# A pipelined attention and mixture-of-experts kernel: score tiles interleaved with the output products, the causal mask moved from TensorE to GpSimd

## The chip, the cores and the metric

The kernel runs on one core of a Trainium2 chip. The metric is the device time of one execution in microseconds (us); smaller is better. Engines are called by the names of the profile: PE is TensorE (PEld its weight loads), DVE is VectorE, ACT is ScalarE, POOL is GpSimd, SP is the engine that issues the transfers.

## What is computed

Two transformer layers over 16 sequences of 512 tokens with 128 features, all in float32:

- Layer 0, attention without softmax (16 heads of 8): `q` and `k` are L2-normalized per head, `out = q (kT v) / scaling`, then the output projection and the residual.
- Layer 0, experts: 8 routed experts of which each token takes 2, and 2 shared ones, with `silu(x w1) * (x w3) w2`.
- Layer 1, attention: `softmax(q kT / sqrt(8))` with a mask, 16 heads of 8. The mask works out as causal: a query sees its own key and all earlier ones, so of the 512x512 scores of a head the part above the diagonal must count as zero.
- Layer 1, experts: RMS norm, a router, each of 16 experts takes the 512 tokens with its highest logits, `gelu`, and a gated scatter back.

## The kernel before

The 16 sequences ("batches") run as a software pipeline. In one pass through the main loop four batches are in work at once, and each engine has its own instruction stream, written out by hand; engines meet at counting semaphores only. `looped` (L262) calls two phases per pass:

- `x_phase(f, b, t, g)`: the ten experts of layer 0 for batch f (`up`, `up3`, `down`), the 40 query-major score tiles of batch b from which DVE takes row maxima (`fill`, `maxima`), the end of layer 1's attention for batch t (`t_turn`, `t_out`, then the residual, the norm and the router logits), and the first norm of batch g.
- `y_phase(b, f, r, t)`: the 40 key-major score tiles of batch b (`pair_scores`, five tiles for a pair of heads) which ACT turns into probabilities (`exps`, L981 to L989), the four products with v (`outputs(0)` to `outputs(3)`, L803, each for four heads, that is two pairs), the layer 0 attention of batch f (`f_kvq`, `f_kv`, `f_kvo`, `f_out`, `f_turn_x1`, `f_gate`), and the query, key and value projections of batch r (`r_turn`, `r_q`, `r_k`, `r_v`).

Score tiles go through three PSUM banks in turn (`ba`), so tile n waits until ACT has read tile n-3. The probabilities have three buffers of five tiles, one for each pair of heads: the exponentials of pair 3 wait for `outputs(0)`, those of pair 5 for `outputs(1)`, those of pair 7 for `outputs(2)`. `outputs(k)` writes the bank `bo`; DVE copies it to `oT` (L1352), PE transposes that back into `bo` (`turn_outputs`, L816), DVE divides by the row sums (`norm`, L1354).

The causal mask is added on PE: after each product for a diagonal block comes one more 128-column matmul of a constant (`mask_k` in L575 for the key-major tiles, `mask_q` in L580 for the query-major ones), which adds a large negative number above the diagonal, so that its exponential is zero:

```
pe.matmul(bank[:, col:col + w], lhsT=KT[0:K_ROWS, head, blk * P:(blk + 1) * P],
          rhs=QT[0:K_ROWS, head, blk * P:], start=True, stop=False)
last = pe.matmul(bank[:, col:col + P], lhsT=identb[:], rhs=mask_k[:], start=False, stop=True)
```

DVE's chain for layer 0's attention starts when ACT has squared q and k (`sq`, L998): `f_l2` sums the squares (L1153) and begins an inverse square root, `f_scale` ends it (three Newton steps of three operations on two halves each, L1160 to L1162, all with both inputs in SBUF) and scales q and k (L1169). In the order of DVE's stream `r_rest` (L1336), `outputs(0)`'s copy and the rest come behind it. POOL in this phase raises variances to the power -0.5 (`power`, L442 to L444) and splits q and k into bf16 parts (L479, L481).

Router logits of batch t: `t_stats`, `t_square` and `t_row` on DVE with two `power` calls of POOL between, then `t_turn_row` and `t_router` on PE (L713, L719) through the bank `bo`, with a copy on ACT between (L971). Before the change all of this lies in `x_phase`. At the end of `x_phase`, `turn_maxima(b, 0)` (L727) transposes the maxima of the first eight heads, ACT copies them, and SP writes them into QT (`max_dmas`, L329); the first score tile of `y_phase` waits for that transfer.

## Time and profile before

| what | value |
|---|---|
| median of 3 runs | 1927.63 us (1927.26 to 1934.12) |
| the profiled execution's own time | 1928.53 us |
| its span, first to last instruction | 1926.7 us |
| PE busy | 1563.0 us, 81% of the span, 10840 matmuls |
| DVE busy | 1219.8 us, 63% |
| ACT busy | 838.3 us, 44% |
| POOL busy | 517.3 us, 27%, 498 instructions |
| mean granted TensorE clock | 0.908 |

The profile gives busy time, but matmuls are pipelined and their ends are modelled, so the distance between two starts tells more than a duration. In the timeline a row is: start, duration, engine, line, operation, output and inputs, and in brackets how long the engine was idle before it and what released it. The main loop takes most of the span; behind it come the selection of tokens and the layer 1 experts, which the change does not touch.

### The profile page before, as it was taken

The numbers are of one execution on the slowest core, as the hardware profiler recorded it, in microseconds if no ns is written. First come the engines' busy times: TensorE is split into PE (matmuls) and PEld (weight loads), VectorE is DVE, ScalarE is ACT, GpSimd is POOL, SyncE is SP. The second block draws the span as 40 slices with busy tenths as digits, with TensorE's granted clock in tenths as the row PEclk, the third lists the DMA queues.
The fourth block names the chain that finished last, engine by engine and source line by source line (L and its number), as shares of the span: only waits on it lengthen the run. The fifth ranks groups of instructions, "written<-read, shape, count | busy, mean of one in ns | idle before, by whom it ended". The sixth has DMA issues, their size and how long they took to land.

```text
span 1926.7 us, 35198 instructions
## 1 busy us (share of the span) xinstructions
PE 1563.0 (81%) x10840; PEld 985.6 (51%) x10840; DVE 1219.8 (63%) x3591; ACT 838.3 (44%) x1755; POOL 517.3 (27%) x498
## 2 busy tenths in 40 slices
PE   3889999899999999898989898989898831257675
PEld 2455555565655555565555555555564421145554
DVE  5566859586868686867767676858583448831111
ACT  0436363635454554545454546353635323423332
POOL 1322212131303131312122222212121020028886
PEclk7879999999999999999999999999999665578978
DMA  2031121303030303030212121121203000034443
GB/s 69 2 76 49 37 64 26 80 9 83 12 77 12 77 12 82 15 74 29 61 39 50 43 46 53 36 53 36 62 22 78 13 12 0 1 66 93 88 89 60
DMA packets 83244, 90.77 MB, mean 47 GB/s; under 512 B 19520, under 2 KB 73024, under 8 KB 78528
## 3 DMA queue, kind: packets, MB, share of 16 engines
q1 hardware_dynamic: 71872, 80.76, 16.7%
q0 software_dynamic: 11264, 8.92, 3.4%
q14 instruction: 84, 0.69, 0.1%
q8 instruction: 24, 0.39, 0.1%
HBM read 58.95 MB, written 29.92 MB: 46 GB/s over the span
## 4 chain that ended last, share of the span: by engine, by line
PE 55%; DVE 18%; issue 12%; POOL 5%; ACT 5%; DMA 3%; DVEq 1%; SPq 1%; ACTq 0%; POOLq 0%
PE fa L666 7%; PE ba L573 6%; PE bo L812 6%; PE fa L660 6%; PE ba L578 5%; PE facc L676 3%; PE fa L676 3%; POOL out L545 2%; PE ba L928 2%; ACT probs L989 2%; DVE passed L1455 2%; PE ba L580 2%; PE ba L575 2%; PE bo L819 2%; DVE nm L1228 1%
## 5 line engine op out<-in xcount | busy, mean ns | idle before, releaser
L989 ACT ACTIVATE probs<-ba 128x512 f32<-128x512 f32 x640 | 330.7, 641 | 103.6 <-PE ba L575 102.8
L450 POOL TENSOR_TENSOR x<-x,gd 128x512 f32<-128x512 f32 x144 | 182.4, 1267 | 675.2 <-ACT gd L964 629.4
L573 PE MATMUL ba<-QT,KT 75*128 75x512 bf16 (+3 forms) x1024 | 253.8, 309 | 39.5 <-ACT probs L989 28.7
L578 PE MATMUL ba<-KT,QT 72*128 72x512 bf16 (+3 forms) x1024 | 248.2, 306 | 18.9 <-DVE nm L1231 12.1
L575 PE MATMUL ba<-mask_k,identb 128*128 128x128 bf16 x1024 | 194.9, 223 | 0.0
L580 PE MATMUL ba<-mask_q,identb 128*128 128x128 bf16 x1024 | 192.8, 223 | 0.0
L1228 DVE TENSOR_REDUCE nm<-ba 128x1 f32<-128x512 f32 x256 | 174.3, 681 | 27.0 <-PE ba L580 26.9
L666 PE MATMUL fa<-f_nT,w 128*128 128x512 f32 x320 | 175.3, 630 | 12.3 <-DVE hh L1220 11.9
L573 PEld LDWEIGHTS ba<-QT,KT 75*128 75x128 bf16 x1024 | 101.5, 99 | 158.5 <-ACT probs L989 107.0
L660 PE MATMUL fa<-f_nT,w 128*128 128x512 f32 x320 | 173.5, 624 | 1.2 <-ACT sc L1020 1.2
L578 PEld LDWEIGHTS ba<-KT,QT 72*128 72x128 bf16 x1024 | 101.1, 99 | 119.5 <-issue 32.3
L812 PE MATMUL bo<-probs,vp 128*32 128x512 f32 (+3 forms) x2048 | 155.2, 445 | 0.8 <-DVE ao L1361 0.8
L957 ACT ACTIVATE sil<-fa 128x512 f32<-128x512 f32 x160 | 95.6, 597 | 110.5 <-PE fa L660 110.5
L1230 DVE TENSOR_REDUCE nm<-ba 128x1 f32<-128x384 f32 x256 | 140.4, 548 | 4.7 <-PE ba L580 4.7
L964 ACT ACTIVATE gd<-facc,gates 128x128 f32<-128x128 f32 x256 | 72.9, 367 | 155.1 <-PE facc L676 155.1
L580 PEld LDWEIGHTS ba<-mask_q,identb 128*128 128x128 bf16 x1024 | 102.0, 100 | 61.2 <-issue 60.0
L1220 DVE TENSOR_TENSOR hh<-sil,fa 128x512 f32<-128x512 f32 x160 | 108.3, 677 | 16.2 <-PE fa L676 8.8
L1352 DVE COPY oT<-bo 128x512 f32<-128x512 f32 x64 | 44.1, 689 | 116.4 <-PE bo L812 115.4
L964 ACT ACTIVATE gd<-fa,gates 128x128 f32<-128x128 f32 x256 | 73.0, 368 | 92.8 <-PE fa L676 92.8
L812 PEld LDWEIGHTS bo<-probs,vp 128*32 128x32 f32 x2048 | 60.9, 111 | 97.6 <-issue 67.0
L1563 DVE TENSOR_TENSOR ysum<-ba,fb 128x512 f32<-128x512 f32 x16 | 11.1, 691 | 155.8 <-PE ba L928 155.8
L545 POOL DMA_INDIRECT out<-contrib,cur x64 | 100.7, 1573 | 30.9 <-issue 18.6
(274 smaller groups left out, 2855.3 us busy)
## 6 DMA issues: line engine op xcount, KB each, us to landing
QT<-qk_parts SPq DMA_DIRECT2D x96, 192.0 KB
KT<-qk_parts SPq DMA_DIRECT2D x96, 192.0 KB
qk_parts<-qkp SPq DMA_DIRECT2D x32, 384.0 KB, 2.5
fc<-in_L_ffn_fc_weight SPq DMA_DIRECT2D x32, 256.0 KB, 3.1
xin<-in_L_attn_x SPq DMA_DIRECT2D x16, 256.0 KB, 7.1
qk_parts<-qkp SPq DMA_DIRECT2D x16, 256.0 KB, 2.7
out<-x SPq DMA_DIRECT2D x16, 256.0 KB, 2.3
xn_rows<-row SPq DMA_DIRECT2D x16, 256.0 KB, 2.4
```

The lines of the kernel that those rows point to most:

```text
L450: pool.tensor_tensor(x1[:], x1[:], gd[:, e % 2], ALU.add).then_inc(S["s_x1g"], 1)
L573: pe.matmul(bank[:, col:col + w], lhsT=KT[0:K_ROWS, head, blk * P:(blk + 1) * P], rhs=QT[0:K_ROWS, head, blk * P:], start=True, stop=False)
L575: last = pe.matmul(bank[:, col:col + P], lhsT=identb[:], rhs=mask_k[:], start=False, stop=True)
L578: pe.matmul(bank[:, col:col + w], lhsT=QT[0:QK_ROWS, head, blk * P:(blk + 1) * P], rhs=KT[0:QK_ROWS, head, 0:w], start=True, stop=False)
L580: last = pe.matmul(bank[:, col + w - P:col + w], lhsT=identb[:], rhs=mask_q[:], start=False, stop=True)
L660: pe.matmul(fa[0][:], lhsT=w1[:, e], rhs=f_nT[:], start=True, stop=True).then_inc(S["s_h1"], 1)
L666: pe.matmul(fa[1][:], lhsT=w3[:, e], rhs=f_nT[:], start=True, stop=True).then_inc(S["s_h3"], 1)
L812: last = pe.matmul(bo[32 * j:32 * j + 32, blk * P:], lhsT=vp[:, blk, 4 * k + j], rhs=prob_block(4 * k + j, blk), start=blk == 0, stop=blk ...
L964: last = act.activation(gd[:, e % 2, q], down_bank(e - 2)[:, q * D:(q + 1) * D], ACT.Copy, scale=gates[:, q, e - 2:e - 1])
L989: act.activation(probs[:, pair % 3, f_], ba[n % 3][:], ACT.Exp, scale=SCALE).then_inc(S["s_exp"], 1)
L1228: last = dve.tensor_reduce(nm[:, 3, h:h + 1], bank[:], X, ALU.max, negate=True)
L1230: dve.tensor_reduce(nm[:, 2, h:h + 1], bank[:, 0:384], X, ALU.max, negate=True)
```

## The change

- PE no longer adds `mask_k`: each key-major block is one matmul, 64 fewer for each batch. Instead POOL zeroes the triangle in the probabilities after the exponential: `cut(b, pair)` issues one `affine_select` for each of the 40 tiles, over 128 columns for tiles 0 and 2 of a pair and over two blocks of 128 columns for the other three. `outputs(k)` waits for these cuts (`s_cut`) instead of the exponentials.
- POOL's other steps of `y_phase` are put between the cuts of its pairs.
- PE's order in `y_phase` is new: score tiles stand between the four parts of an `outputs` step and between the other steps; `turn_maxima(b, 1)` comes after five tiles instead of first.
- `t_stats`, `t_square`, `t_row`, `t_turn_row`, `t_router` and `t_logits` move from `x_phase` to `y_phase`, with buffers of their own and the bank `facc`; `turn_outputs(3)` and `norm(3)` move from the end of `y_phase` into the next `x_phase`.
- The first `up` of `x_phase` waits for the transposed input alone, not for the gate's exponential; `up3` waits for DVE's copy of the gate logits.
- ACT runs a one-column `Exp` at the start of `y_phase` and a one-column `Silu` at the start of `x_phase`.
- On SP `row_dmas` moves between the two halves of `back_dmas`.

```diff
@@ SP, main loop
                 both(max_dmas, i)
+                part_dmas(i + 1)
+                back_dmas(i + 1, 0)
                 row_dmas(i - 1)
-                part_dmas(i + 1)
-                both(back_dmas, i + 1)
+                back_dmas(i + 1, 1)
@@ POOL
+            def cut(b, pair):
+                for f_ in range(5):
+                    pool.wait_ge(S["s_exp"], FILLS * b + 5 * pair + f_ + 1)
+                    apart(pool)
+                    row_ = probs[:, pair % 3, f_]
+                    if f_ in (0, 2):
+                        block_ = row_[:, 0:P]
+                        pool.affine_select(block_, block_, [[1, P]], ALU.is_ge, 0.0, base=0, channel_multiplier=-1).then_inc(S["s_cut"], 1)
+                    else:
+                        apart_by = 384 if f_ < 4 else 256
+                        blocks = row_.rearrange("p (n k) -> p n k", k=P)[:, 0:apart_by // P + 1:apart_by // P]
+                        pool.affine_select(blocks, blocks, [[0, 2], [1, P]], ALU.is_ge, 0.0, base=0, channel_multiplier=-1).then_inc(S["s_cut"], 1)
+
             def y_phase(b, f, r, t):
                 if r is not None:
                     power(b_rs[:], b_ve[:], "s_varb", "s_rsb", r + 1)
-                if r is not None:
-                    for w in range(2):
+                for pair in range(HEADS // 2):
+                    if b is not None:
+                        cut(b, pair)
+                    if r is not None and pair in (1, 2):
+                        w = pair - 1
                         pool.wait_ge(S["s_r1"], 2 * r + w + 1)
...
-                if f is not None:
-                    power(f_rs[:, 0:Q], f_ve[:, 0:Q], "s_varf", "s_rsf", 2 * f + 2)
+                    if t is not None and pair in (3, 4):
+                        power((t_rs, t_rs2)[pair - 3][:], t_ve[:], "s_vart", "s_rst", 2 * t + pair - 2)
+                    if f is not None and pair == 5:
+                        power(f_rs[:, 0:Q], f_ve[:, 0:Q], "s_varf", "s_rsf", 2 * f + 2)
@@ PE, x_phase
                     up3(f, 0)
+                if t is not None:
+                    turn_outputs(t, 3)
                 fill(2)
@@ PE, outputs(k, *beside) and the order of y_phase
-                    pe.wait_ge(S["s_exp"], FILLS * b + 10 * k + 10)
+                    pe.wait_ge(S["s_cut"], FILLS * b + 10 * k + 10)
...
-                    last.then_inc(S["s_pv"], 1)
+                        if blk == Q - 1:
+                            last.then_inc(S["s_pv"], 1)
+                        fills(*beside[blk:blk + 1])
...
+                if_f(f_kvq, 0)
+                fills(0, 1, 2)
+                if_f(f_kvq, 1)
+                fills(3, 4)
+                if_b(turn_maxima, 1)
+                if_r(r_turn)
+                fills(5, 6, 7)
+                if_r(r_q)
+                fills(8, 9, 10, 11)
+                outputs(0, 12, 13, 14)
                 if_r(r_k)
+                fills(15, 16, 17)
+                if_b(turn_outputs, 0)
+                fills(18, 19)
                 if_f(f_kv)
+                fills(20, 21)
+                outputs(1, 22, 23, 24)
+                if_f(f_kvo)
+                if_t(t_turn_row, r)
+                fills(25, 26, 27)
+                if_b(turn_outputs, 1)
+                fills(28, 29)
+                if_f(f_out)
+                fills(30, 31)
+                outputs(2, 32, 33, 34)
+                if_t(t_router)
+                fills(35, 36)
+                if_f(f_turn_x1)
+                fills(37)
+                if_b(turn_outputs, 2)
+                fills(38, 39)
                 if_f(f_gate)
+                if r is not None:
+                    if t is not None:
+                        pe.wait_ge(S["s_l1c"], t + 1)
+                    r_v(r)
+                outputs(3)
@@ ACT, y_phase
                 if b is not None:
+                    act.activation(warm[:], m_b[:, 0:1], ACT.Exp, scale=0.0)
+                exps(0, 4)
+                if b is not None:
                     copy(nmT[:, 1], bo[:].bitcast(BF16)[0:PARTS * HEADS // 2, 0:SEQ], "s_nmt", 2 * b + 2, "s_nmT")
@@ DVE, y_phase
                 if_f(f_l2)
                 if_r(r_rest, 0)
                 if_f(f_scale)
+                if_b(outputs, 0)
                 if_r(r_rest, 1)
-                outputs(0)
-                norm(0)
+                if_t(t_stats)
+                if_b(norm, 0)
                 if_f(f_kvm)
-                outputs(1)
-                norm(1)
+                if_t(t_square)
+                if_b(outputs, 1)
+                if_t(t_row)
+                if_b(norm, 1)
                 if_f(f_x1)
-                outputs(2)
+                if_b(outputs, 2)
+                if_t(t_logits)
```

## Rows read from the trace of the kernel before

**Rows 1.** Chain that ended last, one step in two neighbouring passes: start, us, work

```profile
639.05 2.29 PE bo L812 x32
...
731.16 2.29 PE bo L812 x32
```

**Rows 2.** Busy time by stretch (boundary; y; x): length, busy by engine, clock, DMA

```profile
612.30:616.20 3.90, 3.90 (x22) 3.34 (x20) 0.65 (x4) 1.06 (x2) 1.25 (x1) 0.56 0.01 2
...
613.17:658.73 45.56, 40.85 (x351) 24.49 (x351) 25.17 (x91) 28.83 (x55) 6.83 (x7) 0.97 0.30 76
658.73:705.24 46.51, 43.44 (x266) 27.58 (x266) 42.16 (x112) 16.69 (x45) 14.35 (x12) 0.99 0.08 18
```

**Rows 3.** Timeline of PE, waits and moved steps late in the x phase

```profile
689.35 1.13 PE L666 MATMUL fa<-f_nT,w 128*128 128x512 f32 x2 [0.92 <-DVE hh L1220]
...
696.00 0.28 PE L578 MATMUL ba<-KT,QT 72*128 72x256 bf16 x1 [0.69 <-DVE nm L1231]
...
699.57 0.60 PE L716 MATMUL bo<-ident,row 128*128 128x128 f32 x4
...
702.95 1.07 PE L722 MATMUL bo<-router_w,b_nT 128*128 128x16 f32 x8 [1.21 <-ACT b_nT L971]
```

**Rows 4.** Timeline of PE, a mask matmul and the matmul behind it

```profile
618.61 0.22 PE L575 MATMUL ba<-mask_k,identb 128*128 128x128 bf16 x1
618.67 0.33 PE L573 MATMUL ba<-QT,KT 75*128 75x384 bf16 x1
```

**Rows 5.** Timeline of ACT, the table load and ten exponentials of one y phase

```profile
618.93 1.28 ACT L989 ACT_TABLE_LOAD   x1 [1.52 <-PE ba L575]
...
642.82 5.01 ACT L989 ACTIVATE probs<-ba 128x512 f32<-128x512 f32 x10 [2.70 <-PE ba L575]
```

**Rows 6.** Groups of POOL's instructions by form: busy us, mean ns | idle before

```profile
L493 POOL TENSOR_SCALAR_AFFINE_SELECT earlier_e<-earlier_e 128x128 f32<-128x128 f32 x7 | 2.0, 292 | 1.0
...
L434 POOL TENSOR_SCALAR_AFFINE_SELECT blockdiag<-blockdiag 128x128 f32<-128x128 f32 x1 | 0.4, 408 | 0.1
...
L437 POOL TENSOR_SCALAR_AFFINE_SELECT below<-below 128x64 f32<-128x64 f32 x1 | 0.3, 290 | 0.1
```

**Rows 7.** Timeline behind the main loop, DVE and POOL side by side

```profile
1568.18 0.59 POOL L491 TENSOR_SCALAR_AFFINE_SELECT same_e<-same_e 128x128 f32<-128x128 f32 x1
...
1569.85 1.30 DVE L1420 TENSOR_TENSOR gates<-logits,gmax 128x1024 f32<-128x1024 f32 x1
1570.22 1.09 POOL L491 TENSOR_SCALAR_AFFINE_SELECT same_e<-same_e 128x128 f32<-128x128 f32 x1
```

**Rows 8.** Timeline of DVE in the y phase, the chain of layer 0's attention

```profile
624.24 1.28 DVE L1153 TENSOR_REDUCE n<-sq 128x64 f32<-128x512 f32 x2 [2.26 <-ACT sq L998]
...
629.14 1.27 DVE L1162 SCALAR_TENSOR_TENSOR rn<-rt,rn 128x64 f32<-128x64 f32 x2
...
633.42 0.68 DVE L1352 COPY oT<-bo 128x512 f32<-128x512 f32 x1
```

**Rows 9.** Timeline of POOL in the same y phase

```profile
629.04 1.16 POOL L481 TENSOR_TENSOR qkp<-qkr,qkp 128x512 bf16<-128x512 f32 x1
...
646.79 1.01 POOL L444 TENSOR_TENSOR f_rs<-f_ve,mhalf 128x4 f32<-128x4 f32 x1 [11.31 <-DVE f_ve L1183]
```

**Rows 10.** Timeline of PE in the same y phase

```profile
634.15 0.66 PE L819 MATMUL bo<-ident,oT 128*128 128x128 f32 x4 [1.26 <-DVE oT L1352]
...
638.98 2.36 PE L812 MATMUL bo<-probs,vp 128*32 128x512 f32 x32
```

**Rows 11.** Timeline of DVE, the centred row of the router's input

```profile
694.17 1.11 DVE L1116 TENSOR_SCALAR row<-x,b_mv,b_sc 128x128 f32 x4 [0.19 <-DVE b_sc L1262]
```

**Rows 12.** Timeline of PE at the start of a late y phase

```profile
1449.25 0.61 PE L573 MATMUL ba<-QT,KT 75*128 75x512 bf16 x1 [3.44 <-DMA QT<-nmT]
```

**Rows 13.** Busy time by stretch behind that wait (columns as in rows 2)

```profile
1451.00:1454.00 3.00, 3.00 (x18) 2.20 (x16) 0.60 (x3) 2.66 (x6) 0.00 (x0) 0.50 0.12 36
1454.00:1457.00 3.00, 3.00 (x18) 1.72 (x16) 0.00 (x0) 1.97 (x4) 0.00 (x0) 0.75 0.00 0
```

More of the change, by code:

```diff
@@ L453, in x_phase @@
                 for e in range(U0):
-                    if t is not None and e == 5:
-                        power(b_rs[:], b_ve[:], "s_vart", "s_rst", 2 * t + 1)
                     if g is not None and e == 3:
@@ L463, in x_phase @@
                         pool.tensor_tensor(xres[:], xin[:], b_o0[:, None, :].to_broadcast([P, Q, D]), ALU.add).then_inc(S["s_xres"], 1)
-                    if t is not None and e == 7:
-                        power(b_rs2[:], b_ve[:], "s_vart", "s_rst", 2 * t + 2)
                     if f is not None and e >= 2:
@@ L721, in t_router, with turn_outputs @@
                 for q in range(Q):
-                    last = pe.matmul(bo[:, q * E1:(q + 1) * E1], lhsT=b_nT[:, q * P:(q + 1) * P], rhs=router_w[:], start=True, stop=True)
+                    last = pe.matmul(facc[:, q * E1:(q + 1) * E1], lhsT=rowT[:, q * P:(q + 1) * P], rhs=router_w[:], start=True, stop=True)
                 last.then_inc(S["s_l1"], 1)
-            T_STEPS = {1: t_turn, 2: t_out, 8: t_turn_row, 9: t_router}
+            T_STEPS = {1: t_turn, 2: t_out}
+            def turn_outputs(b, k):
+                pe.wait_ge(S["s_oT"], 4 * b + k + 1)
+                for q in range(Q):
+                    last = pe.transpose(bo[:, q * P:(q + 1) * P], oT[:, q * P:(q + 1) * P], ident[:])
+                last.then_inc(S["s_tr"], 1)
             def turn_maxima(b, half):
@@ L801, in pair_scores, with outputs @@
                         scores(pe, b, n, True)
-                def outputs(k):
-                    pe.wait_ge(S["s_exp"], FILLS * b + 10 * k + 10)
+                def outputs(k, *beside):
+                    if b is None:
+                        return
+                    pe.wait_ge(S["s_cut"], FILLS * b + 10 * k + 10)
                     if k == 0:
@@ L952, in x_phase @@
             def x_phase(f, b, t, g):
+                if f is not None:
+                    act.activation(warm[:], m_b[:, 0:1], ACT.Silu)
                 for e in range(U0):
@@ L980, in y_phase, with exps @@
             def y_phase(b, f, r, t):
-                def exps(pair):
+                def exps(first, last):
                     if b is None:
                         return
-                    for f_ in range(5):
-                        n = 5 * pair + f_
+                    for n in range(first, last + 1):
+                        pair, f_ = divmod(n, 5)
                         act.wait_ge(S["s_st"], FILLS * b + n + 1)
@@ L1294, in x_phase @@
                         maxima(b, n)
+                if t is not None:
+                    norm(t, 3)
                 for e in range(U0):
@@ L1297, in x_phase @@
                         product(f, e)
-                    if t is not None and e in T_STEPS:
-                        T_STEPS[e](t)
+                    if t is not None and e == 3:
+                        t_x3(t)
                     if g is not None and e == 2:
@@ L1370, in if_r, with if_t @@
                         step(r, *w)
+                def if_t(step):
+                    if t is not None:
+                        step(t)
                 if rest:
-                    y_rest(b, f, norm, outputs, if_f)
+                    fc.b = f
+                    if_b(norm, 2)
+                    if_f(f_logits)
+                    if_f(f_gates)
+                    if_f(f_rank)
+                    if_b(outputs, 3)
                     return
                 if_r(r_norm)
-                if_f(lambda f: f_bias(f, 0))
+                if_f(f_bias, 0)
                 if_r(r_center)
-                if_f(lambda f: f_bias(f, 1))
+                if_f(f_bias, 1)
                 if_f(f_l2)
```

186 lines of the change are left out of this document (75 added, 111 removed).

## The prediction, made before the result was known

> **What bounds the kernel now.** I read the chain of waits first, for the rhythm: the same product with v comes back after 92.1 us [rows 1], so one pass of the main loop takes 92.1 us; thirteen such passes and the halves beside them make about 14 that count. Then the busy time by stretch [rows 2]. T is the start of `turn_maxima(b, 0)`. From the first score tile of the x phase to the next T are 46.51 us, in which PE is busy 43.44 and DVE 42.16: PE bounds it, DVE nearly does. From T to the next x phase, 45.56 us, PE is busy 40.85 by a generous measure, DVE 25, ACT 29, POOL 7: nobody is full, so chains decide. In the 3.9 us after the x phase's end the granted clock is 0.56, that is mostly 1.2 GHz instead of 2.4 [rows 2]; before it PE waited 1.21 us for the router's input [rows 3]. The third view is the timeline, engine by engine, of that pass. In it PE waits for DVE's copy of the first output, which comes last in a DVE chain that starts at 624.24 with the sums of squares and reaches the copy at 633.42 [rows 8, 10].
>
> About 0.5%, 10 us, is what a measurement of this kernel can tell from no change. The profiled execution took 1928.53 us, 0.9 above the median of the runs; the sum is made against it.
>
> **The change part by part,** for one pass.
>
> *Masks off PE: 0.* A mask matmul takes 0.06 us from its start to the next one's [rows 4], 64 of them 3.8 us. They are in the y phase, where ten exponentials take 5.01 us, so 0.5 us each [rows 5], while a tile with its masks needs about 0.32 of PE. ACT and DVE's chain cover them. If PE became the bound there, up to 3.8 us would be won; that stays for the range.
>
> *x phase: -3.5.* Out go the row's transposes and the router's matmuls (0.60 and 1.07 by duration [rows 3], 0.43 and 0.91 to the next step's start), in comes one set of output transposes (0.66 by duration [rows 10], 0.44 likewise): -0.9. The router's wait of 1.21 goes. So do the waits of 0.92 and 0.69 for DVE [rows 3], whose cause is the norm work that DVE loses here (1.1 for the row [rows 11], with statistics and small operations some 4, an estimate). The half clock that began inside the x phase cost some 0.5. Against that, DVE arrives at its first maximum about 0.5 later (the gate ranking moves behind the phase's start) and divides the last outputs before the first `hh`: I give 0.8 for `up3` waiting there. Together -0.9 - 2.8 - 0.5 + 0.8, about -3.5; between -2.5 and -4.7.
>
> *T to the first output copy: +1.5.* The table load (1.28, [rows 5]) leaves the path, but tile 3 waits behind the second half of `f_kvq`, and that now for DVE's bias, which stands behind the norm of r: nothing is won, since the squares on ACT, and so DVE's chain, begin where they did. The copy comes ahead of `r_rest(r, 1)`: -0.6. New are the cuts. From the three forms of `affine_select` [rows 6] I work out 0.18 us, 0.79 ns a column and 7 ns a block: 0.29 for 128 columns (as measured) and 0.40 for two blocks; the bounds are 0.29 and 0.63 (half of what a pass of POOL over 512 columns takes, [rows 9]). Five cuts are 1.8 us, 2.1 with issue, less than ACT's 2.5. They meet DVE's chain, though. An `affine_select` of 0.29 took 1.09 while DVE added two tensors from SBUF, and ended with it [rows 7]; a pair of Newton operations on DVE, 629.14 to 630.41, took 1.27 under POOL's subtraction, 629.04 to 630.20, and ended just behind it [rows 8, 9]. The two engines exclude each other there. Cuts 10 to 14 are held up by POOL's bf16 split and then run against twelve Newton operations of some 0.18 us; taking turns, DVE's chain grows by their 1.8 us and by 0.3 from the cuts before: 2.1 - 0.6 = +1.5. If they never meet, -0.6; with dear cuts, +3.
>
> *From that copy to the next x phase: +1.9.* Before: 634.10 to 658.73, 24.6 us [rows 2, 8]. After it, in us from the copy's end: r's rest and POOL's split to 2.5, cuts 15 to 19 to 4.7, so `outputs(1)` at 4.75, as late as it is now (638.98, 4.9, [rows 10]). With its three tiles it ends at 7.7; tile 24 is issued at 7.3, its exponential ends at 8.4, its cut at 8.9. Only then does POOL reach the second power for t (1.0, [rows 9]): 9.95. DVE's row needs 1.5 with its scale factors [rows 11], so PE, which stands at `t_turn_row` since 8.0, goes on at 11.55. Behind that wait are tiles 25 to 39, so ACT stands too. This is a new wait of 3.5 us on the path; now tile 25 starts at 8.2 (`outputs(1)` at 4.9, its 2.3 [rows 1] and `f_out`'s 1.0). What follows is shorter than now (14.5 us against 16.5), because tiles run beside `outputs(2)` and the last turn and the wait for its copy leave: 11.55 + 0.45 + 14.5 = 26.5. Between +0.5 and +3.
>
> *Clock: +0.8.* The boundary's half-clock stretch should go, as PE no longer waits before it; its gain is in the terms above. But a wait of 3.44 us at the start of a late y phase was followed by a granted clock of 0.50 and then 0.75 [rows 12, 13], and 3.5 us at `t_turn_row` is nearest to that row. The boundary's 3.9 us at 0.56 are 3.4 us at half clock, and the same again here would cost 1.7 where PE is the path; ACT's spacing of 0.5 covers half of it. Between 0 and 3.5.
>
> *The rest: 0.* SP's row transfer goes behind the first half of the QT and KT reads; the second half waits for all 40 tiles anyway, some 10 us after the row is ready, and is read only 19 us into the x phase. If the row came later than that, PE would wait at tile 20. The writes for q and k wait for POOL's split behind the cuts, some 2 us later than now, with 20 us to spare. The two one-column activations are 0.2 us on an engine that waits.
>
> The sum is -3.5 + 1.5 + 1.9 + 0.8 = +0.7 us a pass, 14 times +10. Against it, the last x phase, in which DVE has maxima and the norm alone, loses about 4 us of DVE work. 1928.5 + 6 gives 1934 us.
>
> **The rivals.**
>
> *The y phase does not grow (0.30).* POOL's cuts fall between DVE's small operations, and the row arrives while PE still has tiles, or its wait is made good by PE's lighter load. Then the pass is -3.5 - 0.6 + 0 = -4.1, 14 times -57, with the end's -4 1867 us. For it speaks that most time is lost in waits of the y phase and that 3.8 us of PE work go; against it, the exclusion in rows 7 and the order of PE, in which the row's turn stands ahead of 15 tiles.
>
> *The clock falls in the y phase (0.21).* Besides the wait at the row there is one of up to 3.9 us ahead of the first turned output: outputs(0) and tiles 15 to 17 are done long before DVE's copy. If the clock falls at both, each costs the 1.7 us worked out above, on the path: +3.4 instead of 0.8. The pass is then +3.3, 14 times +46, and the time with the end 1971 us. It decides as soon as PE runs at 1.2 GHz through `outputs(1)` or from tile 25 on. Against it stands that the y phase now keeps 0.97 in spite of waits of 1.26 [rows 2, 10]. The Trainium skill (TensorE: Matmul & The Clock Gate, section HAM oscillation) says that a regular wait in each turn of a loop makes PE start every turn cold. By that rule this case is the likely one; rows 12 and 13 agree with it for one wait, rows 10 do not for shorter ones.
>
> *POOL paces the phase (0.07).* If two blocks cost 0.63, five cuts take 2.5 and 0.3 of issue, more than ACT's 2.5. Each of the three later groups of cuts ends 0.7 later: +2.1 on the sum, 14 times 29 us more, 1963 us.
>
> That the masks stay on PE can't be: the code drops them.
>
> **How the numbers follow.** The forecast has 0.42; its own range is 1910 to 1958, of which 0.12 lies below -0.5%, 0.17 within, 0.13 above. With the rivals: faster 0.12 + 0.30 = 0.42, same 0.17, slower 0.13 + 0.21 + 0.07 = 0.41. As cases of both signs hold most of the chance, the range must take in both rivals: from 1850, which leaves out a third of the fast one, to 1985, a third of the slow one.
>
> **What would show it.** The spacing of the same product with v: 92.8 us if I am right, 88 or 95.4 by the rivals. An x phase near 43 us. `oT`'s first copy 1.5 us later after T, with Newton operations of 0.4 us and more beside the cuts. A wait of some 3.5 us of PE at the transposes of the row, ended by DVE. Cuts of 0.29 and 0.40. A granted clock of 1.00 at the boundary and less behind the row's wait. The prediction is wrong if PE does not wait there, if the y phase gets shorter, or if the cuts take more than 0.6.

## The result, and the profile after

| kernel | runs | median us (lowest to highest) | ratio, 95% interval |
|---|---|---|---|
| before | 19 | 1928.20 (1925.32 to 1934.12) | |
| after | 19 | 1937.78 (1932.66 to 1942.25) | 1.0049, 1.0040 to 1.0057 |

The change makes the kernel 9.6 us slower, 0.49% (0.40 to 0.57). That is clear of zero, and just inside the 0.5% that the prediction took for "no change", an outcome to which it gave 0.17. I forecast 1934 us. The sum was nearly right, its parts were not: that shows as soon as one looks at where the time lies.

The profiled execution of after took 1942.25 us with a span of 1940.1; it is the longest of the 19, 4.5 us above their median, and what is read from the profile below divides that execution. Its page, part 1 (busy time) and the clock line of part 2:

```profile
PE 1556.6 (80%) x9816; PEld 920.8 (47%) x9816; DVE 1236.9 (64%) x3591; ACT 856.4 (44%) x1787; POOL 745.1 (38%) x1136
...
PEclk7889989898989999999989898989897665578988
```

PE has 1024 matmuls fewer and its busy time still fell by 6 us only; POOL has gained 228 us. The cuts are these two groups of part 5 (mean ns in the middle):

```profile
L484 POOL TENSOR_SCALAR_AFFINE_SELECT probs<-probs 128x256 f32<-128x256 f32 x384 | 164.0, 430 | 100.2 <-ACT probs L1024 94.3
...
L480 POOL TENSOR_SCALAR_AFFINE_SELECT probs<-probs 128x128 f32<-128x128 f32 x256 | 74.6, 292 | 169.7 <-ACT probs L1024 167.9
```

0.43 and 0.29 us, where I had worked out 0.40 and 0.29 from [rows 6].

To divide the execution I use DVE's addition that ends an x phase. It occurs 16 times; here are its 4th and its 15th start, 11 passes apart, first in the timeline of before, then in that of after:

```profile
340.54 0.69 DVE L1317 TENSOR_TENSOR x<-facc,x 128x512 f32 x1 [2.58 <-POOL x L450]
...
1356.98 0.69 DVE L1317 TENSOR_TENSOR x<-facc,x 128x512 f32 x1 [3.08 <-POOL x L450]
```

```profile
337.97 0.69 DVE L1365 TENSOR_TENSOR x<-facc,x 128x512 f32 x1
...
1352.11 0.69 DVE L1365 TENSOR_TENSOR x<-facc,x 128x512 f32 x1
```

So the profiled span falls into a start (340.5 before, 338.0 after), 11 passes (1016.4 and 1014.1, that is 92.40 and 92.19 a pass) and an end (569.7 and 588.0). Two of before's passes, of 95.30 and 93.48 us, are longer than the other nine (91.66 to 92.08, mostly 92.0); beside those nine a pass of after is about 0.2 longer. **So the loop is hardly slower; the loss, 18.3 us, is at the end.** There the last two y phases run without a batch f and, from the second on, without an r.

Now one pass, cut at the same three points as in the prediction: T, the end of the first output copy, the first tile of the x phase. Columns as in [rows 2]. Before:

```profile
613.17:634.10 20.93, 18.36 (x125) 10.12 (x124) 14.64 (x48) 14.95 (x27) 4.52 (x5) 0.94 0.11 34
634.10:658.73 24.63, 22.50 (x226) 14.38 (x227) 10.52 (x43) 13.88 (x28) 2.31 (x3) 1.00 0.47 112
658.73:705.20 46.47, 43.40 (x265) 27.54 (x264) 42.12 (x112) 16.69 (x45) 14.35 (x12) 0.99 0.08 18
```

After:

```profile
611.47:632.07 20.60, 17.22 (x97) 7.10 (x96) 17.66 (x53) 13.77 (x25) 10.55 (x20) 0.92 0.07 22
632.07:661.10 29.03, 24.78 (x199) 14.52 (x199) 13.09 (x55) 15.52 (x31) 13.25 (x30) 0.88 0.38 92
661.10:703.66 42.56, 41.57 (x260) 26.57 (x256) 37.68 (x96) 17.49 (x46) 11.99 (x10) 1.00 0.14 28
```

The first stretch is 0.33 us shorter, the second 4.40 longer, the third 3.91 shorter: +0.16. In the second one PE is busy longer with fewer matmuls (199 for 226): its granted clock is 0.88 where it was 1.00. The x phase is what it should be, and at its end the clock is 1.00.

What fills the second stretch is seen in PE's timeline of after:

```profile
625.30 1.39 PE L845 MATMUL bo<-probs,vp 128*32 128x512 f32 x8 [0.62 <-POOL probs L484]
...
632.12 0.66 PE L754 MATMUL bo<-ident,oT 128*128 128x128 f32 x4
...
636.56 1.06 PE L845 MATMUL bo<-probs,vp 128*32 128x512 f32 x8 [1.15 <-POOL probs L484]
...
643.72 1.11 PE L740 MATMUL facc<-ident,row 128*128 128x128 f32 x4 [3.00 <-DVE row L1157]
...
661.10 0.39 PE L596 MATMUL ba<-KT,QT 72*128 72x512 bf16 x1
```

PE waits 3.00 us for DVE's row, then runs slower: the same four transposes take 1.11 us where a set takes 0.66 [rows 10]. What DVE did before that row (timeline of DVE):

```profile
640.37 0.69 DVE L1388 COPY oT<-bo 128x512 f32<-128x512 f32 x1 [1.98 <-PE bo L845]
642.12 0.16 DVE L1311 TENSOR_TENSOR t_sc<-t_rs 128x4 f32<-128x4 f32 x1 [1.07 <-POOL t_rs L449]
642.48 1.11 DVE L1157 TENSOR_SCALAR row<-x,t_mv,t_sc 128x128 f32 x4 [0.19 <-DVE t_sc L1311]
```

So the 3.00 us have two parts. DVE's stream has the copy of output 1 ahead of the row, and that copy waits for PE itself; then DVE waits 1.07 us for POOL's power, which stands behind the cuts of tiles 20 to 24.

At the end the same waits return, and there is less beside them that the change makes shorter. PE's timeline of after in the last two y phases:

```profile
1463.68 1.94 PE L845 MATMUL bo<-probs,vp 128*32 128x512 f32 x8 [1.93 <-POOL probs L484]
...
1473.09 1.12 PE L740 MATMUL facc<-ident,row 128*128 128x128 f32 x4 [3.26 <-DVE row L1157]
```

```profile
1546.27 0.66 PE L740 MATMUL facc<-ident,row 128*128 128x128 f32 x4 [3.26 <-DVE row L1157]
...
1560.62 4.01 PE L845 MATMUL bo<-probs,vp 128*32 128x512 f32 x32 [1.61 <-POOL probs L484]
```

Behind the second wait of 3.26 us the transposes still took 0.66; the granted clock was 0.73 from them to 1549.00 and 0.50 in the 3 us after that.

The y phase of batch 14 takes 51.10 us from T to the x phase (1439.71 to 1490.81) where it took 39.55; from T of batch 15 to its last residual 51.01 where it took 41.65; the x phase between them 28.39 where it took 31.81. That is +11.55 - 3.42 + 9.36 = +17.5, nearly all of the loss.

### The profile page after: what moved, and what is told of

Its sections match the earlier page's. It is cut to its first block, busy times and chain, and to the rows that moved or that the text cites. A ratio compares the mean times of both kernels' runs of the same rounds, so it can differ in the third digit from the quotient of the medians.

```text
span 1940.1 us, 34996 instructions
## 1 busy us (share of the span) xinstructions
PE 1556.6 (80%) x9816; PEld 920.8 (47%) x9816; DVE 1236.9 (64%) x3591; ACT 856.4 (44%) x1787; POOL 745.1 (38%) x1136
## 4 chain that ended last, share of the span: by engine, by line
PE 44%; DVE 20%; issue 15%; POOL 9%; ACT 7%; DMA 3%; DVEq 1%; SPq 0%; POOLq 0%; ACTq 0%
PE bo L845 7%; PE fa L686 6%; PE ba L596 6%; PE fa L678 5%; ACT probs L1024 5%; PE ba L592 3%; PE fa L696 3%; PE ba L598 2%; POOL out L564 2%; POOL probs L484 2%; PE facc L696 2%; PE ba L964 2%; DVE passed L1499 2%; DVE nm L1269 2%; DVE f_n L1157 2%
## 5 line engine op out<-in xcount | busy, mean ns | idle before, releaser
L1024 ACT ACTIVATE probs<-ba 128x512 f32<-128x512 f32 x640 | 347.5, 602 | 247.5 <-PE ba L592 247.2
L592 PE MATMUL ba<-QT,KT 75*128 75x512 bf16 (+3 forms) x1024 | 240.3, 337 | 33.1 <-ACT probs L1024 16.7
L845 PE MATMUL bo<-probs,vp 128*32 128x512 f32 (+3 forms) x2048 | 206.4, 495 | 31.8 <-POOL probs L484 31.7
L592 PEld LDWEIGHTS ba<-QT,KT 75*128 75x128 bf16 x1024 | 91.6, 108 | 235.1 <-ACT probs L1024 117.0
L484 POOL TENSOR_SCALAR_AFFINE_SELECT probs<-probs 128x256 f32<-128x256 f32 x384 | 164.0, 430 | 100.2 <-ACT probs L1024 94.3
L480 POOL TENSOR_SCALAR_AFFINE_SELECT probs<-probs 128x128 f32<-128x128 f32 x256 | 74.6, 292 | 169.7 <-ACT probs L1024 167.9
L845 PEld LDWEIGHTS bo<-probs,vp 128*32 128x32 f32 x2048 | 48.0, 113 | 104.5 <-issue 57.3
```

The lines of the kernel that those rows point to most:

```text
L484: pool.affine_select(blocks, blocks, [[0, 2], [1, P]], ALU.is_ge, 0.0, base=0, channel_multiplier=-1).then_inc(S["s_cut"], 1)
L592: last = pe.matmul(bank[:, col:col + w], lhsT=KT[0:K_ROWS, head, blk * P:(blk + 1) * P], rhs=QT[0:K_ROWS, head, blk * P:], start=True, sto ...
L845: last = pe.matmul(bo[32 * j:32 * j + 32, blk * P:], lhsT=vp[:, blk, 4 * k + j], rhs=prob_block(4 * k + j, blk), start=blk == 0, stop=blk ...
L1024: act.activation(probs[:, pair % 3, f_], ba[n % 3][:], ACT.Exp, scale=SCALE).then_inc(S["s_exp"], 1)
```

## Experiments

Eleven more kernels ran. Each was timed beside the kernel before on the same chip; ratios are to that. Apart from "old order, cuts on POOL" each is the kernel after with one or more edits: "row late" is experiment 1, "wait filled" 2, "power first" 3, "masks on PE" and "old order" 4, "split late" 6, "plain outputs" 7, "half the cuts" 8. "Pass" is the mean of the 11 passes of the profiled run, "end" what follows them, both as above.

| kernel | median us | ratio to before, 95% | pass | end |
|---|---|---|---|---|
| after | 1937.78 | 1.0049 (1.0040 to 1.0057) | 92.19 | 588.0 |
| row late | 1859.07 | 0.9639 (0.9617 to 0.9660) | 86.92 | 571.7 |
| power first | 1910.35 | 0.9892 (0.9866 to 0.9919) | 90.59 | 578.1 |
| wait filled | 1937.27 | 1.0048 (1.0031 to 1.0064) | 91.83 | 590.7 |
| new order, masks on PE | 1889.31 | 0.9797 (0.9780 to 0.9813) | 89.65 | 576.1 |
| old order, cuts on POOL | 1946.79 | 1.0114 (1.0080 to 1.0148) | 92.11 | 572.8 |
| row late, masks on PE | 1833.41 | 0.9521 (0.9498 to 0.9544) | 85.59 | 564.3 |
| row late, split late | 1852.91 | 0.9617 (0.9596 to 0.9639) | 86.90 | 564.1 |
| row late, plain outputs | 1844.19 | 0.9578 (0.9555 to 0.9600) | 86.11 | 567.4 |
| row late, half the cuts | 1824.17 | 0.9449 (0.9430 to 0.9468) | 84.71 | 565.0 |
| the same, plain outputs | 1818.54 | 0.9419 (0.9401 to 0.9436) | 84.42 | 562.2 |
| row late, masks on PE, plain outputs | 1811.60 | 0.9386 (0.9368 to 0.9404) | 84.41 | 556.8 |

**1. The row's wait: move the transposes behind 7 more tiles.**

```
                 if_f(f_kvo)
-                if_t(t_turn_row, r)
                 fills(25, 26, 27)
...
                 fills(30, 31)
+                if_t(t_turn_row, r)
                 outputs(2, 32, 33, 34)
```

They are then also behind `turn_outputs(1)` and `f_out`. ACT's copy of the turned row moves with them, from behind exponential 26 to behind 31.

> The changed kernel with one step moved: PE's transposes of the row stand behind score tiles 25 to 31 instead of ahead of tile 25, and ACT's copy of the turned row behind exponential 31 instead of 26. Theory A (PE's wait for DVE's row, 3.0 us in a steady pass and 3.26 in each of the two last y phases, stops the tiles and brings the half clock behind it): the wait goes, the 6.8 us at half clock behind it go too, and a steady pass gets 2.5 to 4 us shorter, the last two y phases 3 to 6 us each: 1938 - 14 x 2.5 to 4 - 6 to 12, so 1870 to 1897 us. Theory B (DVE's f chain, x1 and the gate, sets when the next x phase starts, and PE's tiles only wait beside it): f_x1 comes behind the row on DVE as before, so the steady pass stays within 0.5 us and only the last two y phases, which have no f, win: 1925 to 1935 us. Theory C (POOL's cuts set the pace): the tiles come earlier but their cuts do not; within 0.5% of 1938.

Measured: 1859.07 us, a larger gain than theory A gave: 5.27 us a pass instead of 2.5 to 4. PE's waits for the row, over the whole execution (us in total, times, longest), in after:

```profile
PE facc L740 <- DVE row L1157: 52.4, 16, 6.9
```

and with the row late:

```profile
PE facc L740 <- DVE row L1157: 8.3, 3, 6.9
```

44.1 us of waiting are gone, but 82.1 of the profiled span. Busy time by stretch of a pass with the row late:

```profile
587.81:608.21 20.40, 17.01 (x97) 7.08 (x96) 17.46 (x53) 13.57 (x25) 9.85 (x20) 0.92 0.07 22
608.21:631.98 23.77, 22.22 (x202) 12.58 (x200) 12.96 (x54) 15.71 (x31) 13.19 (x30) 1.00 0.47 115
631.98:674.59 42.61, 41.56 (x260) 26.57 (x256) 37.75 (x96) 17.50 (x46) 11.99 (x10) 1.00 0.13 26
```

Only the second stretch differs from after: 23.77 for 29.03, PE busy 22.22 for 24.78, clock 1.00 for 0.88. The wait took its own length and a slower PE behind it: with the clock's price from experiment 2, 3.00 + 1.72 make 4.72 of the 5.26 us, and where the other half microsecond went was not tried. Theories B and C fall: f's chain on DVE and the cuts followed as soon as the tiles came earlier. At the end 16.3 of the 18.3 us come back too.

**2. The price of the clock: fill the wait with products nobody reads.**

```
             def t_turn_row(t, r):
...
+                for e in range(5):
+                    pe.matmul(facc[:], lhsT=w1[:, e], rhs=w1[:, 0:4], start=True, stop=True)
                 pe.wait_ge(S["s_row"], t + 1)
```

The wait for the bank, which stood behind the one for the row, goes ahead of the products.

> The changed kernel with five 128x128x512 float32 products, which nothing reads, put on PE ahead of its wait for the row (0.6 us each by the rows of the same shape in the x phase, together 3.0, which is the length of the wait). It asks for the price of the clock alone: the wait is filled, and nothing that waits for it starts earlier. If the half clock behind the row's wait costs time (my prediction gave it 0.8 us a pass), the granted clock behind the row stays at 1.00 and the pass gets 1 to 2 us shorter: 1910 to 1924 us. If ACT's spacing of 0.5 us covers it, or the half clock comes from elsewhere, no change or some longer because the five products overrun the wait: 1936 to 1950 us.

Measured: 1937.27 us, inside the range of the second theory (1936 to 1950). That theory allowed for two reasons, that the half clock costs nothing or that the products overrun the wait, and the total can't tell them apart. The stretch can. From the row's transposes to the x phase, in after and then in this kernel (columns as in [rows 2]):

```profile
643.72:661.10 17.38, 17.38 (x136) 11.00 (x137) 7.31 (x33) 9.29 (x18) 6.22 (x16) 0.82 0.34 74
```

```profile
639.63:655.29 15.66, 14.88 (x138) 8.72 (x136) 7.40 (x33) 9.17 (x18) 6.44 (x16) 1.00 0.34 74
```

The same work takes 17.38 us at a granted clock of 0.82 and 15.66 at 1.00: a difference of 1.72 us a pass. By itself that could hold something besides the clock, since the stretch starts later here and what PE waits for had more time; experiment 3 has stretches of one kernel, behind waits of one length, that differ in the clock, and gives 1.6. The products overran the wait, though (timeline of PE in this kernel):

```profile
635.34 4.46 PE L739 MATMUL facc<-w 128*128 128x512 f32 x10
639.63 0.60 PE L742 MATMUL facc<-ident,row 128*128 128x128 f32 x4
```

The transposes came 12.79 us behind the end of the first copy and not 11.65 as in after, which gives 1.14 of the 1.72 back; the pass gains 0.36 and the end loses 2.7. So the median stood still because the products overran, not because the clock is free. The Trainium skill (TensorE: Matmul & The Clock Gate, section HAM oscillation) says of a loop in which PE waits for a transfer in each turn that every turn then starts cold; these two stretches agree with it, for a wait of 3.00 us for another engine.

**3. The length of the wait: POOL's part alone.**

```
+                    if t is not None and pair == 4:
+                        power(t_rs2[:], t_ve[:], "s_vart", "s_rst", 2 * t + 2)
                     if b is not None:
                         cut(b, pair)
```

> The changed kernel with POOL's second power for t ahead of the cuts of tiles 20 to 24 instead of behind them; nothing else moves. DVE's square is done near 638.4 in the pass read, so the power ends near 639.4 and not at 642.1, and DVE's row then waits only for its copy of output 1. It takes POOL's part (1.07 us) out of PE's wait of 3.00 us and leaves DVE's part (1.9). Theory A (the wait costs its length, and the half clock behind it stays): 1.1 us a pass, with the two last y phases 16 x 1.1 = 17, so 1918 to 1923 us. Theory B (the wait costs more than its length because the half clock behind it goes with a shorter wait): 1.1 + 1.7 us a pass, 1890 to 1900. Theory C (cuts 20 to 24 come a microsecond later and outputs(2) waits for them): no gain, 1934 to 1942.

Measured: 1910.35 us, 1.60 a pass, between A and B. PE's timeline shows the wait of the size that was left, DVE's part:

```profile
631.45 1.11 PE L742 MATMUL facc<-ident,row 128*128 128x128 f32 x4 [1.84 <-DVE row L1159]
```

It is 1.16 us shorter, and of this length in every pass of the loop. The clock behind it is not the same in every pass. From the transposes to the x phase, in three of the passes (columns as in [rows 2]):

```profile
270.87:286.84 15.97, 14.98 (x137) 8.96 (x137) 7.29 (x32) 9.18 (x18) 6.44 (x16) 1.00 0.46 100
631.45:647.83 16.38, 16.12 (x137) 9.93 (x137) 7.41 (x33) 9.28 (x18) 6.30 (x16) 0.90 0.41 91
993.44:1011.03 17.59, 17.59 (x136) 11.01 (x137) 7.38 (x33) 9.29 (x18) 6.29 (x16) 0.81 0.38 85
```

Of 13 such stretches one has 1.00, nine have 0.89 or 0.90 and last 16.09 to 16.44 us, three have 0.81 and last 17.58 to 17.71. The kernel and the wait are the same in all, so the clock of 0.81 costs 1.6 us here, and that of 0.90 some 0.1 to 0.5. In after all 13 have 0.81 to 0.83. So of the 1.60 us that a pass gains, some 1.1 are the wait's length, and the rest goes with a clock that fell for a shorter time: a mixture of A and B. Theory C falls: outputs(2) waited 0.25 us for its cuts.

**4. The two halves of the change, apart.** New order with `mask_k` on PE again and `outputs(k)` waiting for `s_exp`, no cuts; and the old order with the cuts:

```
-                    last = pe.matmul(bank[:, col:col + w], lhsT=KT[...], rhs=QT[...], start=True, stop=True)
+                    pe.matmul(bank[:, col:col + w], lhsT=KT[...], rhs=QT[...], start=True, stop=False)
+                    last = pe.matmul(bank[:, col:col + P], lhsT=identb[:], rhs=mask_k[:], start=False, stop=True)
...
-                    pe.wait_ge(S["s_cut"], FILLS * b + 10 * k + 10)
+                    pe.wait_ge(S["s_exp"], FILLS * b + 10 * k + 10)
```

> The order of the changed kernel with the masks left as matmuls on PE and no cuts on POOL: outputs(k) wait for the exponentials alone. It takes the reordering without the second half of the change. PE gains 64 x 0.06 = 3.8 us of work in a y phase; POOL loses 15.1 us a pass (24 cuts of 0.43 and 16 of 0.29). If the cuts are what sits on the path (power of t behind cut 24, outputs(1) 1.15 us behind its cuts, Newton steps on DVE beside cuts): 1 to 2 us shorter a pass, 1905 to 1925 us. If PE's load is: up to 3.8 us longer a pass, up to 1990 us. If both are beside the path, within 0.5% of 1938.

> The order of the kernel before with the second half of the change alone: no mask matmuls on PE, cuts on POOL, outputs(k) waiting for the cuts. If the cuts cost nothing beside DVE and PE's 3.8 us are not on the path (my prediction's 0 for the masks): within 0.5% of 1928. If PE's load was on the path in the old order: up to 3.8 us shorter a pass, down to 1880. If the cuts stand in the way (DVE's chain and the wait of outputs(k) for the last cut, 0.5 to 1 us at each of four outputs): 2 to 4 us longer a pass, 1956 to 1985 us.

Measured: 1889.31 us, below the 1905 to 1925 that were expected if the cuts are on the path, and 1946.79 us, in none of the three ranges. So everything but the cuts, the new order with the moved steps, wins 2.0%, and the cuts on top of it lose 2.6% (1937.78 by 1889.31). In the old order the cuts lose 1.1% (0.8 to 1.5) by the median. Stretches of a pass with the new order and the masks on PE:

```profile
595.12:615.03 19.91, 17.39 (x125) 8.77 (x124) 16.77 (x54) 14.67 (x27) 4.45 (x5) 1.00 0.07 23
615.03:642.02 26.99, 25.09 (x234) 15.88 (x235) 12.91 (x57) 14.89 (x29) 4.79 (x5) 0.94 0.40 98
```

The new order has a wait for the row even without cuts (timeline of PE):

```profile
624.66 0.93 PE L742 MATMUL facc<-ident,row 128*128 128x128 f32 x4 [1.84 <-DVE row L1159]
```

Stretches of the old order with the cuts:

```profile
619.47:641.05 21.58, 18.59 (x97) 8.05 (x96) 15.57 (x47) 14.41 (x27) 9.84 (x20) 0.87 0.11 33
641.05:664.74 23.69, 20.56 (x191) 12.07 (x191) 10.73 (x43) 14.44 (x30) 10.96 (x28) 1.00 0.48 115
```

In the new order the cuts cost 0.69 us up to the first copy (20.60 against 19.91) and 2.04 from there on. In the old order they cost 0.65 up to the copy, as there, and give 0.94 back behind it, where PE has fewer matmuls; there is no row in that phase for POOL to hold up. So that pass is as long as most of before's. It belongs to the fastest of four executions, 1934.23 us, though. The other three took 1942.87, 1950.70 and 1956.72, and the mean granted clock falls as the time grows: 0.892, 0.888, 0.884, 0.879, where before has 0.907 to 0.910. What lowered it stays open, as the three left no trace.

**5. The fourth corner: row late and masks on PE.** Both edits together.

> The row's transposes late, and the masks left as matmuls on PE without cuts on POOL: the fourth corner of a square with the changed kernel (pass 92.2 us, 1938), the row late alone (86.6, 1859) and the masks on PE alone (89.2, 1889). Theory A (the cuts cost the path only through the row: POOL's second power waits behind cut 24, which adds 1.07 us to the wait for the row, and outputs(1) waits 1.15 for its cuts): with the row out of the way the cuts' price falls from 3 us a pass to about 1, while PE gets 3.8 us of mask work back, so the pass is 86 to 87.5 us and the time 1850 to 1875. Theory B (the two effects are separate and add): 86.6 - 3.0 = 83.6 us a pass, 1815 us. Theory C (with the row's wait gone PE's load is the path): up to 3.8 us longer a pass than the row late alone, 1890 to 1912.

Measured: 1833.41 us, 85.59 a pass, between A and B. With the row late a pass pays 1.33 us for the cuts (86.92 - 85.59), with the row early 2.54 (92.19 - 89.65). So about half of the cuts' price came through the row and half did not. Theory C falls: PE does 3.8 us more work in the phase, and the pass is shorter.

**6. Where the other half lies: POOL's split for k behind the cuts of pair 3.**

```
-                    if r is not None and pair in (1, 2):
-                        w = pair - 1
+                    if r is not None and pair in (1, 3):
+                        w = pair // 2
```

> The row late, and POOL's bf16 split for k (0.61 + 1.16 us) behind the cuts of tiles 15 to 19 instead of ahead of them. In the run with the row late these cuts are held by the split until 700.92 and outputs(1) waits 1.15 us for them; the exponentials were done at 699.07. Theory A (that wait is on the path): outputs(1) starts 1.1 us earlier and less of the phase runs at half clock: 1 to 1.8 us a pass, 1833 to 1845 us. Theory B (DVE's chain from the statistics to the row or f's chain takes the gain back): 0 to 0.4 us a pass, 1853 to 1860. A loss is possible if the writes for k come late enough for the x phase: PE would wait at tile 0 or 20 of the x phase.

Measured: 1852.91 us, 6 less than with the row late, with intervals that overlap. The wait of 1.15 us at outputs(1) did go:

```profile
697.52 1.07 PE L845 MATMUL bo<-probs,vp 128*32 128x512 f32 x8
```

The pass is the same, 86.90. Single passes were as short as 85.7, others 88 and more, some with waits that had not been there, such as this one, early in an x phase, for DVE's copy of output 3:

```profile
634.56 0.65 PE L754 MATMUL bo<-ident,oT 128*128 128x128 f32 x4 [1.56 <-DVE oT L1388]
```

In the mean of the 11 passes the stretch from the first copy to the x phase is 0.57 us shorter (22.99 for 23.56) and the x phase 0.55 longer (43.12 for 42.57). So theory B holds for the loop: what outputs(1) gains, DVE's later copies take back. The gain is in the end (564.1 for 571.7).

**7. The tiles between the steps of outputs(0) to (2), put behind them.**

```
-                outputs(0, 12, 13, 14)
+                outputs(0)
+                fills(12, 13, 14)
```

and likewise for outputs(1) and (2).

> The row late, and score tiles 12 to 14, 22 to 24 and 32 to 34 behind outputs(0), (1) and (2) instead of between their steps. Theory A (the tiles between the steps give ACT work while PE multiplies, and so help): three times outputs(k) of 2.3 us in which ACT gets nothing, some of it covered: 1 to 4 us longer a pass, 1875 to 1915. Theory B (they only move work inside PE's queue, and make each output 1.4 us later for DVE's copy): no change or up to 2 us shorter a pass, 1830 to 1860. In the last two y phases, which have no f, A expects them longer and B shorter than with the row late alone (44.9 and 47.1 us from T to the end).

Measured: 1844.19 us. Theory A falls: the interleaving does not help, it costs 0.8 us a pass and 4.3 at the end. Up to the first copy little changes (20.41 to 20.75 us behind T; 20.40 to 21.11 with the row late alone), since outputs(0) ends earlier but DVE's chain does not, and PE stands for the copy instead of running through:

```profile
688.76 0.66 PE L754 MATMUL bo<-ident,oT 128*128 128x128 f32 x4 [2.22 <-DVE oT L1391]
```

**8. Towards a better kernel.** Row late, masks of tiles 0 to 19 on PE and cuts for tiles 20 to 39 only, with both forms of outputs; and all masks on PE with plain outputs.

> The row late; the masks of tiles 0 to 19 as matmuls on PE, the cuts of tiles 20 to 39 on POOL. In the run with the row late and all masks on PE (85.6 us a pass, 1833) PE is busy through the phase; up to outputs(1) POOL's split and powers and DVE's chain stand beside the cuts, behind it POOL has two powers only. Theory A (a cut costs only where POOL or DVE's chain is on the path, the first half, and a mask on PE costs where PE is, the second half): the first output copy stays at T + 19.9, and from it to the next x phase 32 x 0.06 = 1.9 us of PE go: 83.7 to 84.8 us a pass, 1806 to 1823 us. Theory B (in the second half f's chain on DVE and the last cuts set the end): 85.3 to 86.5 a pass, 1829 to 1850.

> The same with tiles 12 to 14, 22 to 24 and 32 to 34 behind outputs(0), (1), (2) instead of between their steps. With the row late alone this took 1859 to 1844: the steady pass 86.6 to 86.0, and the last two y phases with what lies between them 13 us less from x2 of the last batch to its x3... the half of the gain each. If that adds here: 10 to 16 us less than the half cuts alone. If PE, now with masks in the first half, has no waits left that the earlier copy could use: within 4 us of the half cuts alone.

> The row late, all masks on PE, and the tiles behind the outputs instead of between their steps. Against the row late with all masks on PE (1833 us): 0 to 15 us less if the plain order's gain with the row late (15 us) does not depend on the cuts; 0 to 20 us more if ACT, which gets no tile during an output, runs dry now that PE's tiles take 0.32 us each.

The second of these expectations misread its rows: of the 16 us that plain outputs gained, some 12 were there by the last batch's addition and 4 came behind it, not 13.

Measured: 1824.17, 1818.54 and 1811.60 us. Between the steps, half the cuts beat all masks on PE (84.71 a pass for 85.59), as theory A said, whose pass was right (83.7 to 84.8) and whose time was just missed (1806 to 1823): a cut costs where POOL's split and DVE's chain stand, and behind them it is cheaper than the mask. That holds for the interleaved form only. With plain outputs both give 84.4 a pass, and the kernel without cuts wins 7 us, 5.4 of them at the end. The other two expectations missed: plain outputs gave 5.6 us with half the cuts, neither 10 to 16 nor less than 4, and 21.8 us with the masks on PE, more than the 15 allowed. The kernel without cuts is the fastest one, 6.1% below before. One of its passes by stretch:

```profile
659.13:679.04 19.91, 16.63 (x125) 9.12 (x124) 16.76 (x54) 15.16 (x28) 4.43 (x5) 1.00 0.07 23
679.04:701.17 22.13, 22.08 (x235) 15.45 (x235) 12.59 (x55) 13.37 (x27) 4.79 (x5) 1.00 0.49 120
701.17:743.70 42.53, 41.58 (x261) 26.59 (x257) 37.65 (x96) 17.49 (x46) 12.00 (x10) 1.00 0.13 28
```

Its granted clock is 1.00 throughout, PE is busy 22.08 of 22.13 us and 41.58 of 42.53; only in the stretch up to the first copy does PE still wait, 1.32 us of it for DVE's copy. What it keeps of the change is the order and the moved row; the cuts and the tiles between the output steps are out.

## Why the prediction was right, and where its steps were not

The time, 1934 us for 1937.78, came out by luck, because errors of opposite sign met: over the 11 passes the forecast of +0.7 each gave +7.7 us and -2.3 were measured, while the end came out 18.3 us longer instead of a little shorter. By its steps:

- **Masks off PE: 0.** Not borne out. In the old order it is seen to hold only in the profiled execution (92.11 a pass, and 92.0 in most of before's); by the median the cuts lose 1.1% there. In the new order the cuts that take the masks' place cost 2.5 us a pass (experiment 4). About half of that came through the row, behind POOL's power (experiment 5); the rest lies with the cuts of tiles 0 to 19 (experiment 8), 0.69 of it ahead of the first copy.
- **x phase: -3.5.** Right: -3.91. PE's idle time there fell from 3.07 to 0.99 us and its busy time by 1.83, where I had -2.0 for waits with the delay at `up3`, and -1.4 for work and clock. Which step gave how much was not tried by itself.
- **T to the first copy: +1.5.** Wrong: -0.33. The order alone gave -1.02 (19.91 for 20.93), more than my -0.6, and the cuts +0.69 instead of +2.1. The mechanism was right in direction: see the rows below. But "taking turns, DVE's chain grows by their 1.8 us" was too dear: the chain from the sums of squares to the copy grew by 0.81 us (9.04 for 8.23 with the masks on PE).

DVE's timeline of after, in the chain ahead of the first copy, and POOL's beside it:

```profile
624.27 0.58 DVE L1201 SCALAR_TENSOR_TENSOR rt<-n,rn 128x64 f32<-128x64 f32 x2
624.77 0.56 DVE L1202 TENSOR_TENSOR rt<-rt,rn 128x64 f32<-128x64 f32 x2
625.25 0.41 DVE L1203 SCALAR_TENSOR_TENSOR rn<-rt,rn 128x64 f32<-128x64 f32 x2
...
628.49 0.69 DVE L1201 SCALAR_TENSOR_TENSOR rt<-n,rn 128x64 f32<-128x64 f32 x2
...
629.97 1.50 DVE L1210 TENSOR_TENSOR kvq<-kvq,rn 128x512 f32<-128x512 f32 x2
```

```profile
624.36 0.89 POOL L484 TENSOR_SCALAR_AFFINE_SELECT probs<-probs 128x256 f32<-128x256 f32 x2 [0.67 <-ACT probs L1024]
...
628.44 0.41 POOL L484 TENSOR_SCALAR_AFFINE_SELECT probs<-probs 128x256 f32<-128x256 f32 x1
...
629.98 1.76 POOL L484 TENSOR_SCALAR_AFFINE_SELECT probs<-probs 128x256 f32<-128x256 f32 x2 [0.87 <-ACT probs L1024]
```

The scaling with the masks on PE:

```profile
613.14 1.29 DVE L1212 TENSOR_TENSOR kvq<-kvq,rn 128x512 f32<-128x512 f32 x2
```

A pair of Newton operations takes 0.41 us where it meets no cut; three pairs took 0.58, 0.56 and 0.69, and the scaling 1.50 where it took 1.29 with the masks on PE. That is 0.15 to 0.28 us for each meeting, not the whole cut of 0.29 to 0.43. In the last meeting POOL paid more than DVE: two cuts took 1.76 us, where the two at 624.36 took 0.89. The prediction let DVE pay for every cut. The Trainium skill (SBUF — State Buffer, section Who interferes with whom) says that a DVE instruction with two inputs in SBUF contends with a POOL instruction that reads SBUF; these rows agree that such a meeting costs.

- **From that copy to the next x phase: +1.9.** Wrong: +4.40, which holds the clock too, where the sum had 1.9 and 0.8 for the clock. The steps up to the wait were close: outputs(1) 4.49 us behind the copy (I had 4.75), the row's transposes 11.65 (11.55), a wait of 3.00 (3.5). "11.55 + 0.45 + 14.5" is the term that failed: what followed took 17.38 instead of 14.95. 1.6 to 1.72 of it is the clock, by experiments 2 and 3; the other 0.7 or so is an error of this term that was not traced.
- **Clock: +0.8.** Mis-sized, in its length. I took 3.4 us at half clock, which would cost 1.7 with PE on the path, and let ACT's spacing cover half. Behind the row's wait a mean of 0.82 over 17.38 us makes 6.3 us at half clock, worth 3.1 by the same reckoning, and 1.6 to 1.72 showed in the time: about half was covered, as I had allowed. Both of the clock rival's places did fall below full clock: 0.92 up to the first copy, 0.88 behind it. The first of them did not lengthen the pass by its 1.7: the stretch is 0.33 us shorter than before, and what the cuts added to it is in DVE's chain. There was no long wait ahead of the first turned output: outputs(0) itself, between tiles and partly at the lower clock, took 5.15 us (625.30 to 630.45), so PE had nothing left to wait for at 632.12.
- **The pass: +0.7.** Measured +0.16 in the pass read, and -0.2 in the mean of 11, as two passes of before were 1.5 and 3.3 us longer than the others.
- **The end: "its -4".** This is the step that failed most. The last x phase did lose 3.4. But I carried the steady pass's cover to a place where it does not exist: the y phases of batches 14 and 15 have no f, so nothing there was won for the row, the longer outputs and the clock, and I counted none of them there. These two phases are 21 us longer. The runs divide the end's 18.3 us in part: without the cuts it is 11.9 us shorter (576.1 for 588.0), with the row late 16.3 shorter, with both 23.7.

Of the rivals, the one in which the y phase does not grow needs what experiment 1 made: with the row out of the way the second stretch is 23.77, below 24.63, and the kernel 3.6% faster; its time of 1867 was near to the measured 1859. The order of PE, "in which the row's turn stands ahead of 15 tiles", was the reason against it, and it was the right one. POOL does not pace the phase: two blocks took 0.43 us and not 0.63, and with the row late POOL is busy 23 of 44 us. The bound of 0.63 was misread as well: half of the 1.16 us in [rows 9] is 0.58. Of the signs that the prediction named, the wait of PE at the row, the cuts, the x phase and the clock at the boundary came as said; the later first copy did not.

## What to carry to other kernels

A step that is moved into another phase brings its wait along: on an in-order engine, ask what stands behind it in the queue and put it as late as its reader allows. Here seven score tiles and two other steps between the row and its transposes were worth 4.1%. A wait costs more than its length when the clock falls behind it, and a gain that rests on cover in the steady loop has to be summed again for the first and last turns, in which part of that cover is missing. Handing small work from the busiest engine to an idle one is no gain by itself: PE's 0.06 us a mask was cheaper than POOL's 0.29 to 0.43 us a cut in the first half of the phase, where other work of POOL and DVE stood beside the cuts, and in the second half at best 0.9 us a pass was won (84.71 for 85.59).

## What the runs showed that was not expected

- With the row late, 64 matmuls more on PE in each pass make the pass shorter, 85.59 us for 86.92. With plain outputs, 32 of them in place of 20 cuts left the pass alone (84.41 and 84.42).
- The clock fell behind short waits too: in after PE's three waits of 0.55, 0.57 and 0.62 us ahead of outputs(0) were followed by products at a lower clock (0.92 in that stretch). With the same order and the masks on PE, where PE waited 0.43 and 0.51 us there and did 28 matmuls more in that stretch, it stayed at 1.00.
